# Half of one subtraction of the edge loop moved from VectorE to GpSimd, in a graph network layer with a routed feed-forward layer behind it

## The reference, cut to what matters

```python
h        = mish(concat(x[src], x[dst], edge_attr) @ W1 + b1)
messages = mish(h @ W2 + b2)
agg      = segment_sum(messages, dst)          # into 1250 rows
u        = mish(concat(x, agg) @ W3 + b3)
x        = x + layernorm(x + u @ W4 + b4) * gamma + beta   # here the inner x is normalised
x        = x + routed_ffn(layernorm(x))        # 16 experts, top 2
```

## Time and profile before

| | |
|---|---|
| median of three runs | 1312.96 us |
| the profiled execution | 1314.14 us |
| its span, first to last instruction | 1312.5 us |
| PE, DVE, ACT, POOL busy, share of the span | 86%, 79%, 66%, 47% |
| line 813, count and median | 83 times, 1218 ns |
| mean granted clock of PE | 0.928 |

### The profile page before, as it was taken

The page is one execution under the profiler, slowest core; times in us unless marked ns, Lnnn a source line. Parts: engine busy times, 40 slices in busy tenths (PEclk is TensorE's granted clock), DMA queues, the critical chain, the costliest instruction groups (busy, mean ns, idle before and its releaser), DMA issues. The chain is left out here.

```text
span 1312.5 us, 20757 instructions
## 1 busy us (share of the span) xinstructions
PE 1132.8 (86%) x5823; PEld 904.6 (69%) x5824; DVE 1039.3 (79%) x1793; ACT 863.3 (66%) x1061; POOL 623.2 (47%) x506
## 2 busy tenths in 40 slices
PE   0983799999999999999999999999479995679972
PEld 0762677777777877777777777777257764568851
DVE  2831399999999999999999999999737775643373
ACT  1310498888988888888889898889434441433340
POOL 1332666666666666666566666662021110644410
PEclk9997799999999999999999999999779995689965
DMA  5443766666666666666666666664010112634452
GB/s 148 150 175 86 155 133 127 127 122 127 124 128 124 127 126 124 128 125 128 126 128 125 129 123 126 124 121 108 0 64 25 47 36 97 196 88 128 128 187 84
DMA packets 137304, 153.47 MB, mean 117 GB/s; under 512 B 79293, under 2 KB 87884, under 8 KB 137129
## 3 DMA queue, kind: packets, MB, share of 16 engines
q0 software_dynamic: 40912, 101.69, 37.5%
q1 hardware_dynamic: 96281, 50.65, 14.5%
q10 hardware_dynamic: 16, 0.02, 0.0%
HBM read 141.73 MB, written 15.66 MB: 120 GB/s over the span
## 5 line engine op out<-in xcount | busy, mean ns | idle before, releaser
L696 POOL DMA_INDIRECT gath<-dst_table,idx_sl x166 | 302.5, 1822 | 50.6 <-issue 50.6
L706 POOL DMA_INDIRECT gath<-src_table,idx_sl x166 | 192.5, 1160 | 257.2 <-PE ps L823 190.2
L828 PE MATMUL ps<-W2h,hTh 128*128 128x512 f32 x664 | 262.7, 396 | 0.0
L828 PE MATMUL ps<-W2l,hTh 128*128 128x512 f32 x664 | 262.3, 395 | 0.0
L828 PE MATMUL ps<-W2h,hTl 128*128 128x512 f32 x664 | 188.6, 405 | 0.0
L828 PEld LDWEIGHTS ps<-W2l,hTh 128*128 128x128 f32 x664 | 124.8, 188 | 29.4
L828 PEld LDWEIGHTS ps<-W2h,hTh 128*128 128x128 f32 x664 | 125.4, 189 | 23.1
L726 ACT ACTIVATE act<-ps 128x1024 f32<-128x1024 f32 x83 | 85.3, 1028 | 60.7 <-issue 41.1
L828 PEld LDWEIGHTS ps<-W2h,hTl 128*128 128x128 f32 x664 | 112.9, 188 | 15.6
L763 DVE TENSOR_TENSOR agg<-agg,ps 125x512 f32 x166 | 113.3, 683 | 13.1 <-PE ps L864 2.5
L734 ACT ACTIVATE act<-act 128x1024 f32<-128x1024 f32 x83 | 88.1, 1061 | 40.9 <-DVE act L792 39.0
(11 more groups left out here) (314 smaller groups left out, 2540.3 us busy)
## 6 DMA issues: line engine op xcount, KB each, us to landing
f_w_raw<-in_L_ffn_w_dram SPq DMA_DIRECT2D x32, 512.0 KB, 4.5
ea_sl<-ea_scr SPq DMA_DIRECT2D x332, 32.0 KB
ea_scr<-in_edge_attr_dram POOLq DMA_DIRECT2D x1, 5000.0 KB
w_raw<-in_L_gnn_W_dram SPq DMA_DIRECT2D x3, 1024.0 KB, 18.7
idx_sl<-idx_scr SPq DMA_DIRECT2D x166, 1.5 KB
gath<-src_table,idx_sl POOLq DMA_INDIRECT x166
gath<-dst_table,idx_sl POOLq DMA_INDIRECT x166
x_raw<-in_x_dram SPq DMA_DIRECT2D x5, 500.0 KB
```

The lines of the kernel that those rows point to most:

```text
L696: pool.indirect_dma_start(out=gath[:, k, j, :], out_offset=None, in_=dst_table[:, :], in_offset=bass.IndirectOffsetOnAxis(ap=idx_sl[:, p % ...
L706: pool.indirect_dma_start(out=gath[:, k, j, :], out_offset=None, in_=src_table[:, :], in_offset=bass.IndirectOffsetOnAxis(ap=idx_sl[:, p % ...
L828: return nc.tensor.matmul(ps_2[:, p % 2, j, :], part[:, p % 2, d, j * P:(j + 1) * P], weights[:, d, :], start=False, stop=last)
```

## The change

Line 813 subtracts only the first of the pair's two tiles on DVE, 128x512 elements. POOL gets the second, in each step after its four gathers. The semaphore `msg_lo_ready` becomes two, one for each half, and both readers (ACT before it overwrites `act2`, PE before line 864's product) wait for both. On POOL the new instruction waits for `msg_hi` of its pair and, from the third pair on, for the sums of two pairs before, whose `msg_lo` it overwrites.

```diff
@@ gpsimd, per step, behind the gathers of line 706
+                p = s - 3
+                if exists(p):
+                    pool.wait_ge(S["msg_hi_ready"], p + 1)
+                    if p >= 2:
+                        pool.wait_ge(S["sum_ps"], p - 1)
+                    nc.gpsimd.tensor_tensor(msg_lo[:, p % 2, 1], act2[:, p % A2, 1], f32(msg_hi[:, p % 2, 1]), ALU.subtract).then_inc(S["msg_lo1_ready"], 1)
                 for w in pool_parts.get(s, ()):
@@ scalar, before line 731
-                        act.wait_ge(S["msg_lo_ready"], g - A2 + 1)
+                        act.wait_ge(S["msg_lo0_ready"], g - A2 + 1)
+                        act.wait_ge(S["msg_lo1_ready"], g - A2 + 1)
@@ vector, line 813
-                    nc.vector.tensor_tensor(msg_lo[:, f % 2], a3, f32(msg_hi[:, f % 2]), ALU.subtract).then_inc(S["msg_lo_ready"], 1)
+                    nc.vector.tensor_tensor(msg_lo[:, f % 2, 0], a3[:, 0], f32(msg_hi[:, f % 2, 0]), ALU.subtract).then_inc(S["msg_lo0_ready"], 1)
@@ tensor, before line 863
-                    pe.wait_ge(S["msg_lo_ready"], m + 1)
+                    pe.wait_ge(S["msg_lo0_ready"], m + 1)
+                    pe.wait_ge(S["msg_lo1_ready"], m + 1)
```

More of the change, by code:

```diff
@@ L648, in edge_phase @@
         names = ("dst_ready eaT_ps eaT_hi eaT_lo gath_read lin1_ps exp1 inc1 sq1 ln1 quot1 h_ready h_hi h_lo lin2_ps "
-                 "exp2 inc2 sq2 ln2 quot2 msg_ready msg_hi_ready msg_lo_ready onehot_ready sum_ps summed w3_in w3_hi w3_lo").split()
+                 "exp2 inc2 sq2 ln2 quot2 msg_ready msg_hi_ready msg_lo0_ready msg_lo1_ready onehot_ready sum_ps summed w3_in w3_hi w3_lo").split()
         S = {n: sem("e_" + n) for n in names}
```

## The result

The changed kernel takes 1353.75 us, the median of four runs, against 1312.26 us for the kernel before beside it: a ratio of 1.0314, 95% interval 1.0295 to 1.0332. It is 41 us slower. The forecast was 1284 us with a range to 1318; the first rival said 1357.

A forecast was written before the change was run, and what follows sets the result against it. DVE was taken to set the pace at 9.453 us a step, with PE close at 9.02. 78 x (9.453 - 9.06) = 30.7 us, less 1, off 1314.14 us gave 1284 us, range 1277 to 1318.

The forecast's parts named there:

- the first rival: Edge loop: POOL gets in ahead of DVE's line 805, which stands still about 1.2 us every step; 1357 us, chance 20%.
- What bounds the kernel: Even part of the edge loop: DVE sets the pace at 9.453 us a step, PE close behind at 9.02.
- What is removed: Half of line 813 saves DVE 0.54 us a step, list 8.91 us; PE limits the gain to 0.43 us.
- POOL's room: POOL's gathers plus the subtraction take 8.56 to 8.76 us of a 9.02 us step, leaving 0.3 to 0.5 us.
- the late gathers: POOL's queue: target gathers held behind the new wait end at 516.37, PE wants them at 520.62; 4.2 us of cover.
- The contention: POOL's subtraction kept out until line 805 ends at 510.78, then costs DVE 0.10 us at line 813; step 9.06 us.
- rows 9: Prologue profile rows: six DVE instructions keep their pace, while one of two POOL copies, 0.61 us alone, takes 3.38 us.
- The point of return: DVE's loss per step above which the change no longer gains: 0.43 + 0.11 = 0.54 us.
- The ends of the loop: Before 168 us and in the drain: +1 us, from -1.5 to +3.

The follow-up runs named there:

- DVE's half alone: Changed kernel without POOL's subtraction, the second half of msg_lo set to zero once ahead of the loop: 1286.76 us, ratio 0.9799 to the kernel before.
- the quarter: Changed kernel with POOL subtracting only 256 of its 512 columns, the other 256 set to zero once: 1307.93 us, ratio 0.9965 to the kernel before.
- the probes: Kernel before plus short DVE instruction trains ahead of the edge loop, POOL released within them, three runs; in the first, tensor_scalar trains ran 1.06 us too long.
- the fastest kernel: Changed kernel with POOL's subtraction also waiting for the end of DVE's hTl subtraction in the same step: 1279.57 us, ratio 0.975 to the kernel before.

## Why the prediction was wrong, by its own steps

**What bounds the kernel: right.** DVE sets the pace and PE stands 0.43 us behind it. Once DVE's list fell short enough, the step went to 9.029 us, against 9.02 read from one early step in the earlier trace rows. Two small readings were off and changed nothing. DVE's timeline isn't quite without gaps: before the second 763 it is idle for 0.12 us, and the 8.91 us hold that time. And a wait that empties a pipeline would be worth more than its 0.49 us to PE, not 0.43; the two numbers come from different steps, and no run separates them.

**What is removed: right.** 0.60 us from start to start for the half. DVE's half alone gave 0.33 us a step and not 0.43, as a second cast met a gather; with both stretches DVE's list is 9.11 us. I had named 9.11 as an upper end, but from another sum (9.01 + 0.1), so that the two agree is chance.

**POOL's room, and the late gathers: right.** The subtraction works for 1.27 us. The four gathers are longer than the 6.99 us of the earlier trace rows, 2.37 + 1.79 + 1.04 + 1.41 us with three gaps of 0.30 = 7.51, and still POOL has 0.6 us left to wait in each step of the changed kernel. The cover of 4.2 us for gathers held back behind a wait was enough: the kernel that holds them back most is the fastest.

**The contention: the step that failed.** I wrote that I take it "that POOL is kept out until 510.78, as in rows 9". POOL was kept out only to the end of the instruction that ran when it asked. It asked during inc2, got in at its end, and hTl then stood still and lost 1.11 us, where my sum had 0.10 us for DVE. The runs show it from four sides: hTl at 2.3 us in the changed kernel and 1.21 with POOL behind it; 1.22 with an instruction of POOL that only writes; half the loss for half the columns; and the whole loss gone with work on DVE in that place that reads one input from PSUM. The earlier trace rows had shown the right rule, a POOL instruction (an addition, which I called a subtraction) that got in between two of DVE's, and the earlier trace rows the exception. I had both before me and took the one whose DVE instruction was of line 802's kind.

**The rival: right in mechanism and nearly in size.** 1357 us against 1353.75; 10.0 us a step against 9.951. I summed 8.91 - 0.2 for the cast + 1.27 - 0.07 to 9.9. In the profile it is 8.91 - 0.20 + 1.11 = 9.82; 0.06 for the `hTh` cast, which takes 0.75 us beside a gather, makes 9.88, and most of the rest is idle time of DVE, on average 0.16 us more ahead of its first sum addition and 0.10 us less ahead of the second. The point of return, 0.54 us lost on DVE, was nearly met by the quarter. Its chance was set too low: 20% on the say of one row against another.

**The Trainium skill,** "SBUF — State Buffer", "Who interferes with whom": that a DVE instruction with two SBUF inputs contends with a GpSimd instruction that reads SBUF, and not with one that only writes, agrees with 2.31 against 1.22 us here. The page doesn't say whether a train of DVE instructions back to back counts as one holder; the probes say it doesn't.

**The ends of the loop.** I allowed -1.5 to +3 us. The changed kernel's part behind the last of these subtractions is 0.4 us shorter than before, and the fastest kernel's 0.4 us longer.

## What to carry to other kernels

When work moves from DVE to POOL, find the DVE instruction that will run at the moment POOL is released, and the one behind it: in these runs the latter paid nearly POOL's whole working time if it was a subtraction with both inputs in SBUF or a 128x1024 tensor_scalar within SBUF (1.11 and 1.06 us for 1.27), and nothing if it read one input from PSUM or was a reduction. One copy in the prologue went the other way, so look at the trace of the changed kernel before you trust this. A semaphore that releases POOL in the midst of DVE's list fixes that meeting in every step, so choose it by what DVE does next and not by when the data is ready; here one more wait turned +3.1% into -2.5%. And where two rows of a profile speak against each other, the sum hangs on something that neither has settled: give both nearly the same chance, or find a third.

## What was not expected of the hardware

The same 1.27 us of POOL cost DVE 1.11 us, 0.25 us or next to nothing, by position alone. Indirect gathers and casts that lie beside each other are stretched at some offsets and not at others, without any semaphore between them: between 300 and 800 us a target gather takes from 1.54 to 2.57 us over these runs, a cast of 128x1024 from 0.68 to 0.97. So taking work off POOL altogether (1286.76 us) was worse than leaving it there in the right place (1279.57 us), because it moved the gathers under the casts.
